# Moving two pieces of work in an audio tower kernel: the centring of the next group's tokens, and the transposes of a tile's results

## The reference

```
h = einsum('bpk,kd->bpd', patches, W) + b                      # 128 x 92 tokens of width 128
x = layernorm(h)                                               # (x - mean) / sqrt(var + eps)
s_a = einsum('bhie,bhje->bhij', k, q) / e;  attn = softmax(s_a)
ax = einsum('bhtf,bhit->bhfi', v, attn);  h = h + (ax rearranged) @ Wlt
t = layernorm(h);  gates = softmax(t @ Wr + br);  the top 2 gates, scaled to the sum 1
out = sum over experts e of combine[:, e] * (relu(t @ W1[e] + b1[e]) @ W2[e] + b2[e]);  h = h + out
```

## Time and profile before

| | |
|---|---|
| median of 3 runs | 1559.43 us (1559.01 to 1562.08) |
| the profiled execution | 1560.75 us, with a span of 1558.7 us |
| PE busy | 1402.7 us (90%) |
| DVE busy | 1185.0 us (76%) |
| ACT busy | 1018.3 us (65%) |
| POOL busy | 802.7 us (51%) |
| stage one | to about 850 us from the span's start |
| stage three | about 1154 to 1498 us |

### The profile page before, as it was taken

The page is one execution under the profiler, slowest core; times in us unless marked ns, Lnnn a source line. Parts: engine busy times, 40 slices in busy tenths (PEclk is TensorE's granted clock), DMA queues, the critical chain, the costliest instruction groups (busy, mean ns, idle before and its releaser), DMA issues.

```text
span 1558.7 us, 31914 instructions
## 1 busy us (share of the span) xinstructions
PE 1402.7 (90%) x7926; PEld 1136.2 (73%) x7926; DVE 1185.0 (76%) x3077; ACT 1018.3 (65%) x2282; POOL 802.7 (51%) x886
## 2 busy tenths in 40 slices
PE   4899999999999999999998999999849999999940
PEld 3677877787787788778776777777648888888830
DVE  1889898989889898988996788888736666666643
ACT  1587877877787787777785777777625555555510
POOL 1466343434434443443442577777735556666665
PEclk8999999999999999999998999999969999999975
DMA  3322222222222222222224788767356777666768
GB/s 81 129 74 89 74 96 83 88 82 78 87 73 90 89 88 81 79 87 73 87 92 173 254 273 278 258 228 249 145 203 243 249 251 248 244 245 243 250 207 309
DMA packets 114774, 247.45 MB, mean 159 GB/s; under 512 B 15376, under 2 KB 70816, under 8 KB 111776
## 3 DMA queue, kind: packets, MB, share of 16 engines
q1 hardware_dynamic: 92912, 206.43, 37.2%
q0 software_dynamic: 14368, 32.25, 6.4%
q10 hardware_dynamic: 7440, 8.15, 1.5%
HBM read 100.78 MB, written 90.43 MB: 123 GB/s over the span
## 4 chain that ended last, share of the span: by engine, by line
PE 66%; DVE 14%; issue 7%; DMA 7%; POOL 3%; ACT 2%; SPq 1%; DVEq 0%; POOLq 0%; ACTq 0%
PE bank L333 14%; PE bank L335 13%; PE bank L334 13%; PE bank L1393 7%; PE bank L1326 5%; PE bank L1418 4%; DVE w2s L1075 2%; PE bank L1458 2%; DMA hch<-h_scratch 2%; DVE probT_l L1068 2%; DMA sorted_scratch<-trow,posi 2%; DVE sixes L980 2%; PE bank L1543 2%; PE bank L1316 2%; PE bank L1568 2%
## 5 line engine op out<-in xcount | busy, mean ns | idle before, releaser
L592 POOL TENSOR_TENSOR prob<-expo,inv 92x368 f32<-92x368 f32 x256 | 204.6, 799 | 448.2 <-DVE inv L1054 448.2
L734 POOL DMA_INDIRECT y_scratch<-ytok,tin x212 | 204.9, 967 | 154.4 <-DVE ytok L1278 89.5
L1269 DVE SCALAR_TENSOR_TENSOR hid_l<-bank,hid_h 128x512 fp32r<-128x512 f32 x212 | 146.6, 692 | 130.2 <-ACT hid_h L921 130.2
L921 ACT ACTIVATE hid_h<-bank 128x512 fp32r<-128x512 f32 x212 | 126.8, 598 | 146.5 <-PE bank L335 146.5
L709 POOL DMA_INDIRECT sorted_scratch<-trow,posi x184 | 180.5, 981 | 68.2 <-issue 52.2
L1047 DVE TENSOR_REDUCE peak<-bank 92x4 f32<-92x368 f32 x256 | 136.1, 532 | 89.5 <-PE bank L1393 89.3
L1393 PE MATMUL bank<-z,xnT 128*92 128x368 f32 x512 | 200.5, 473 | 0.0
L781 ACT ACTIVATE z<-bank 128x368 f32<-128x368 f32 x256 | 122.2, 477 | 66.5 <-PE bank L335 59.4
L819 ACT ACTIVATE w2s<-bank 128x368 fp32r<-128x368 f32 x256 | 122.5, 479 | 62.1 <-PE bank L335 58.6
L826 ACT ACTIVATE expo<-cent 92x368 f32<-92x368 f32 x256 | 129.8, 507 | 26.0 <-DVE cent L1059 23.5
L1075 DVE TENSOR_TENSOR w2s<-bank,w2s 128x368 fp32r<-128x368 f32 x256 | 136.1, 531 | 6.3 <-ACT w2s L819 2.4
(11 more groups left out here) (192 smaller groups left out, 3810.1 us busy)
## 6 DMA issues: line engine op xcount, KB each, us to landing
ax_scratch<-val SPq DMA_DIRECT2D x64, 736.0 KB, 3.5
arow<-ax_scratch SPq DMA_DIRECT2D x23, 2048.0 KB
w1t<-w1s SPq DMA_DIRECT2D x53, 512.0 KB, 3.5
w2t<-w2s SPq DMA_DIRECT2D x53, 512.0 KB, 3.0
tin<-sorted_scratch SPq DMA_DIRECT2D x53, 260.0 KB, 3.0
xin<-in_x_dram SPq DMA_DIRECT2D x32, 372.0 KB
arow<-y_scratch SPq DMA_DIRECT2D x24, 256.0 KB, 8.9
h_scratch<-hT SPq DMA_DIRECT2D x32, 184.0 KB, 7.1
```

Of the source, the lines that this page charges most:

```text
L592: nc.gpsimd.tensor_tensor(prob[:, k % 2], expo[:, k % 2], inv[:, k % 2].unsqueeze(2).to_broadcast([S, HH, S]), ALU.mult).then_inc(prob_kep ...
L734: pool.indirect_dma_start(out=y_dram, out_offset=bass.IndirectOffsetOnAxis(ap=tin[:, b, r, D:D + 1].bitcast(I32), axis=0), in_=ytok[:, b % ...
L1269: V.scalar_tensor_tensor(hid_l[:, f], hid_ps[f][:], 0.0, hid_h[:, f].bitcast(F32), ALU.max, ALU.subtract).then_inc(hidl_kept, 1)
```

## The change

Two moves; no operation is added, removed or resized.

1. DVE's `keep_xcent(g + 1)` in step 2 stood right behind `keep_var`, ahead of `probT_l` and `mix_l`. It now stands behind both of them.
2. PE's `turn_y(n - 1)` stood behind `second_layer(n, 0)` and `first_layer(n, 3)`. It now stands right behind `turn_tile(n + 1)`, ahead of both.

```
                 if k == 2 and exists(g + 1):
                     keep_var(g + 1)
-                    keep_xcent(g + 1)
                 gt, kt = back(g, k, LAG_TK)
...
                 if k == 1 and exists(g + 1):
                     keep_sixes(g + 1)
+                if k == 2 and exists(g + 1):
+                    keep_xcent(g + 1)
                 if k == 4 and exists(g + 1):
                     keep_xnl(g + 1)
...
                 if is_tile(n + 1):
                     turn_tile(n + 1, i, q + 1)
+                if is_tile(n - 1):
+                    turn_y(n - 1, past_q % 2)
                 if now:
                     second_layer(n, i, q, 0)
                     first_layer(n, i, q, 3)
-                if is_tile(n - 1):
-                    turn_y(n - 1, past_q % 2)
-                if now:
                     second_layer(n, i, q, 1)
```

## The result

The changed kernel takes 1542.78 us (median of 4 runs, 1540.97 to 1544.20); the kernel before, run beside it, 1560.64 (4 runs, 1559.01 to 1562.08). The ratio is 0.9885, with a 95% interval of 0.9868 to 0.9902: faster by 1.15%, about 18 us. The forecast was 1546.4 with 1541.0 to 1551.5, so the time lies in the range and in the direction given, 3.6 us under the number: it fell on the first rival, a stage three that costs next to nothing.

What follows compares the result with a forecast made beforehand. The prediction took PE's wait for DVE's `mix_l` to bound stage one and PE alone stage three. It summed -18.0 + 4.0 + 0.1 + 0.9 = -13.0 us, from 1559.43 to 1546.4 us, range 1541 to 1551.5.

Steps and rivals of the forecast that it cites:

- the first rival: Stage three: the new wait of `turn_y` costs next to nothing, -16.6 us in all, 1542.8 us; chance 0.15.
- What bounds the kernel: Stage one: PE waits for DVE's `mix_l`, 0.68 us a group; stage three: PE alone sets the pace, busy 310.0 of 310 us.
- Move one, 18.0 us: Stage one, step 3: `xcent` behind `mix_l` gives back 0.60 us of PE's wait in each of 30 groups.
- The 0.27 us to spare in step 4: Stage one: step 4's mix, 0.60 us sooner, still finds its `mix_l` in time by 0.27 us, so the gain passes.
- the rival with a wait that takes over part: Stage one, step 3 to step 5: the chain holds 0.2 of the 0.6 us, gain 12, 1552.4 us; chance 0.14.
- Its bounds: Move one: at most the whole wait of 0.68 us a group, 20.4 us; at least 0.
- The cover for `xtok` and `prob`: Stage one, POOL: both come later, but PE transposes them over a microsecond after they start; cost 0.
- Move two, eight together cost what four and four cost: Stage three, PE: each transpose costs its successor's load, 0.11 us, whoever the successor is; gain 0.
- Move two, the wait in the loop, 4.0 us: Stage three: `turn_y` waits for ACT's `yT`, losing 0.095 us a tile in 42 loop tiles; 0.4 to 7.6 us.
- The end, +0.9 us: Last tile: `turn_y` waits 0.46 us for `yT`, and the transposes delay `first_layer` piece 3 by another 0.44.
- The clock: Stage three: PE's clock falls from 1.00, costing 4 us or more for each tile at the lower level; chance 0.02.
- the rival's 1566 us: Stage three: the kernel's time if PE's clock falls for five tiles, 1546.4 + 20; chance 0.02.

Runs made afterwards that it cites:

- e6: The changed kernel with `turn_y` ahead of `turn_tile`, so that it must wait for `yT` in every tile: 1567.25 us, ratio 1.0019 to the kernel before.
- e1: The kernel before with move one only, `xcent` behind `mix_l` and `turn_y` at its old place: 1542.92 us, ratio 0.9872 to the kernel before.
- e4: The changed kernel with the moments and `varA` put behind `mix_l` too: 1532.08 us, ratio 0.9808 to the kernel before.
- e7: The changed kernel with `xcent` one step later, behind `mix_l` of step 3: 1579.81 us, ratio 1.0101 to the kernel before.
- e2: The kernel before with move two only, `turn_y` right behind `turn_tile`: 1562.56 us, ratio 0.9996 to the kernel before.
- e8: The changed kernel with `turn_y` between `second_layer(n, 0)` and `first_layer(n, 3)`, apart from the other transposes: 1544.99 us, ratio 0.9882 to the kernel before.
- e9: The version with moments, `varA` and `xcent` behind `mix_l`, but `turn_y` at its old place: 1533.64 us; the same with the new place, run beside it: 1534.86.
- e10: The changed kernel with `xcent` back ahead of `probT_l` and `mix_l`, and `varA` behind them instead: 1545.45 us, ratio 0.9885 to the kernel before.
- e3: The kernel before with `xcent` put between `probT_l` and `mix_l`: 1564.24 us, ratio 1.0008 to the kernel before.
- e5: The changed kernel with `varA` behind `mix_l` too, the moments left ahead: 1532.41 us, ratio 0.9798 to the kernel before.

## Why the prediction was right, and where it was not

- **What bounds the kernel.** Right. In stage one PE lost its time behind `mix_l`, and a DVE instruction moved out of that queue came back as PE's time one for one. In stage three PE alone sets the pace: e6's wait came back as 0.43 us a tile.
- **Move one, 18.0 us.** Right: 0.586 for each of 29 groups in the trace, 24.28 us a group where 24.3 was said, stage three 18.0 us sooner, and e1 shows that it is the whole gain. The 0.27 us to spare in step 4 was enough; the rival with a wait that takes over part is refuted by the group of 24.28.
- **Its bounds.** The lower held. The upper, 0.68 us, was mis-read: the stall was 0.91, as e4 shows. In the list of waits the prediction took PE's row (16.4 us) and passed over the larger row of the weight loads (30.5 us). It did not hurt the forecast, since `xcent` holds only 0.60 of the queue, but it hid that another 0.3 us a group was to be had.
- **The cover for `xtok` and `prob`.** Right, shown by the rows after and by e7.
- **Move two, eight together cost what four and four cost.** Right within what can be timed (e2, e8, e9). The trace has 0.027 us a tile in favour, 1.4 us over 51 tiles, which the sum did not have.
- **Move two, the wait in the loop, 4.0 us.** This is the term that was mis-sized. It came from the middle between 0.05 and 0.22 us for the time from ACT's end to PE's load. In the change it is 0.04 to 0.06 in every tile and in e6 0.04 or 0.05, both in the loop. The row with 0.22 was the wrong one to take. In the same trace, one group later, the same load starts 0.05 after `z` ends (429.81 and 429.86):

```profile
429.33 0.48 ACT L781 ACTIVATE z<-bank 128x368 f32<-128x368 f32 x1
...
429.86 0.44 PEld L1316 LDWEIGHTS bank<-ident,xin 93*128 93x128 f32 x4
```

The two kinds take turns from group to group (six of each between 200 and 500 us). So a load in a hardware loop can follow ACT by 0.05, and the other 0.17 us have another cause, which the profile calls "issue" and which stays open. The term should have been 0 to 0.5 us, and the forecast would have been 1542.8, that of the first rival.

- **Luck in the number.** That 1542.8 is the time measured to a tenth is luck. Stage three became 0.7 us shorter, where the first rival has it 1.4 longer (0.5 and 0.9), and the kernel before took 1560.64 us beside the change, 1.2 more than the 1559.43 of the forecast. The measured gain is 17.9 us, 18.7 in the profiled executions; 13.0 was forecast and the first rival has 16.6.
- **The end, +0.9 us.** Right in kind, 0.72 measured between the last two `yT`.
- **The clock.** The granted clock of stage three stayed at 1.00, the 2.4 GHz level, with eight transposes side by side, 0.8 us of a tile of 6.36. The Trainium skill (TensorE: Matmul & The Clock Gate, Part 4: PE-mode transpose) says that transposes do not count as TensorE's activity in the same way as matmuls; what that rule would have made of this kernel, the rival's 1566 us, did not come.

## What to carry to other kernels

When PE waits for one engine in order, list everything that stands in that engine's queue ahead of what PE waits for, and ask of each piece who needs it and when; what has a microsecond of cover belongs behind. Measure the stall by the distance between two starts against the same distance where nothing waits, and end it at the second matmul behind the wait. PE's idle bracket leaves out what the modelled end of a matmul covers; look at the row of the weight load too. For a wait that is a tie, look at more than one pair of the same two engines before choosing a time between them, and test it by moving the instruction to where it must wait.

## What the runs showed of the hardware that was not expected

`varA` is a VectorE instruction on 92x4 values. With nothing of POOL beside it, it takes 0.15 to 0.17 us (the rows of e4 and e10). In its old place it takes 0.55, and it ends with POOL's product: in the group of the changed kernel shown above, 416.67 + 0.56 = 417.23 and 416.41 + 0.80 = 417.21. Near the start of stage one, where POOL also prepares weights, it takes 1.78 us. These are rows of the changed kernel:

```profile
98.24 0.80 POOL L592 TENSOR_TENSOR prob<-expo,inv 92x368 f32<-92x368 f32 x1 [1.66 <-DVE inv L1054]
98.51 1.78 DVE L991 TENSOR_SCALAR varA<-moments 92x4 f32<-92x4 f32 x1
99.00 1.26 POOL L652 TENSOR_TENSOR arow<-arow,w2room 127x512 f32<-127x512 f32 x1
...
101.33 0.41 PE L333 MATMUL bank<-probT_h,xtok_h 92*128 92x368 f32 x1 [1.61 <-DVE w2s L1074]
```

It stays through the whole of `prob` and then of `arow` and ends 0.03 us after `arow` (100.29 and 100.26), and PE's row behind it has an idle time of 1.61 us. `xcent`, which reads PSUM, kept its 0.68 us in the same place beside the same product (e10). Nor is every small instruction beside POOL held up: `inv`, also 92x4 and started at 419.54 while `xtok` ran (418.80 to 419.84), took 0.16 us. This fits what the Trainium skill says of the port pair that VectorE and GpSimd share (SBUF — State Buffer, section "SBUF: two separate sides"): the pair is locked for a whole instruction and the other side blocks fully, but on VectorE's side this concerns only instructions in a two-port mode or with two inputs in SBUF. In which mode `varA` ran, no run shows. The lock itself is argued from the coinciding ends; what the runs show is that in a steady group `varA` is held up in one place and not in the other, and that moving it is worth 0.46 us a group.

Some distances of groups near the start are 26.26 us in the kernel before and up to 27.90 in executions of e2 and e3, where a steady group takes 24.86; in e5 they are under 24.9. That such groups come and go may be part of why executions of the kernel before differ, by 3 to 14 us within a set of runs; it was not tried and is not shown.
